# K and V products of a cross-attention by Strassen's scheme over pairs of batches

## The reference

```python
q = x @ Wq + bq
kv = context @ Wkv + bkv
k, v = jnp.split(kv, 2, axis=-1)
...
q = _larope(q, Lq)
k = _larope(k, Lk)
scores = jnp.einsum('bhqd,bhkd->bhqk', q, k) * SCALE
scores = jnp.where(context_mask[:, None, None, :], scores, -jnp.inf)
attn = jax.nn.softmax(scores, axis=-1)
out = jnp.einsum('bhqk,bhkd->bhqd', attn, v)
out = out.transpose(0, 2, 1, 3).reshape(B, Lq, H * hd)
return out @ Wo + bo
```

## Time and profile before

| | us |
|---|---|
| median of 3 runs | 776.84 (775.82 to 777.03) |
| the profiled execution | 779.38 |
| its span, first to last instruction | 777.6 |
| PE / DVE / ACT / POOL busy | 751.2 / 500.9 / 418.6 / 336.6 |
| mean granted TensorE clock | 0.985 of full speed |

### The profile page before, as it was taken

The page is one execution under the profiler, slowest core; times in us unless marked ns, Lnnn a source line. Parts: engine busy times, 40 slices in busy tenths (PEclk is TensorE's granted clock), DMA queues, the critical chain, the costliest instruction groups (busy, mean ns, idle before and its releaser), DMA issues. The chain is left out here.

```text
span 777.6 us, 23428 instructions
## 1 busy us (share of the span) xinstructions
PE 751.2 (97%) x9650; PEld 665.3 (86%) x9651; DVE 500.9 (64%) x1209; ACT 418.6 (54%) x978; POOL 336.6 (43%) x366
## 2 busy tenths in 40 slices
PE   8999999999999999999999999999899999599997
PEld 7899999999999999998999989997677777488784
DVE  6776765666575585675666557656889998622236
ACT  5465656556565566656656556664466664033330
POOL 1655456455454455544555445531133221246640
PEclk9989999999999999999999999999999999689999
DMA  8504010110011110011001100201942238634448
GB/s 294 208 29 164 27 40 29 36 57 30 29 36 36 49 37 29 32 33 57 30 29 49 44 30 29 83 29 57 408 174 110 105 122 350 207 114 166 162 140 319
DMA packets 23174, 77.96 MB, mean 100 GB/s; under 512 B 3328, under 2 KB 4736, under 8 KB 20128
## 3 DMA queue, kind: packets, MB, share of 16 engines
q1 hardware_dynamic: 19392, 64.45, 23.1%
q0 software_dynamic: 3680, 12.06, 4.7%
HBM read 57.89 MB, written 18.61 MB: 98 GB/s over the span
## 5 line engine op out<-in xcount | busy, mean ns | idle before, releaser
L164 PE MATMUL bank<-chi,wparts 128*128 128x258 f32 x496 | 143.2, 289 | 0.5 <-DVE v L759 0.5
L166 PE MATMUL bank<-chi,wparts 128*128 128x258 f32 x496 | 139.9, 282 | 0.0
L165 PE MATMUL bank<-clo,wparts 128*128 128x258 f32 x496 | 139.8, 282 | 0.0
L392 POOL TENSOR_TENSOR ksin<-kb,const 128x516 f32<-128x516 f32 x64 | 93.4, 1460 | 101.1 <-ACT kb L505 101.0
L505 ACT ACTIVATE kb<-bank,bias_cols 128x258 f32<-128x258 f32 x126 | 60.0, 476 | 66.4 <-PE bank L166 66.4
L412 POOL TENSOR_TENSOR ctx_sums<-craw 128x512 f32<-128x512 f32 x30 | 39.5, 1315 | 128.2 <-DVE ctx_sums_lo L776 128.2
L164 PEld LDWEIGHTS bank<-chi,wparts 128*128 128x128 f32 x496 | 93.8, 189 | 1.1 <-DVE v L759 0.7
L165 PEld LDWEIGHTS bank<-clo,wparts 128*128 128x128 f32 x496 | 94.1, 190 | 0.0
L166 PEld LDWEIGHTS bank<-chi,wparts 128*128 128x128 f32 x496 | 93.8, 189 | 0.0
L748 DVE TENSOR_TENSOR kcos<-kb,const 128x516 f32<-128x516 f32 x64 | 51.0, 798 | 29.6 <-ACT kb L505 29.6
L510 ACT ACTIVATE pr<-pr,nmax 128x257 f32<-128x257 f32 x128 | 63.5, 500 | 5.8 <-DVE nmax L784 5.8
(11 more groups left out here) (380 smaller groups left out, 2243.9 us busy)
## 6 DMA issues: line engine op xcount, KB each, us to landing
craw<-ctx_t_dram SPq DMA_DIRECT2D x32, 516.0 KB, 3.5
expert_lo<-weights_dram SPq DMA_DIRECT2D x8, 1024.0 KB, 12.5
expert_hi_scratch<-wraw SPq DMA_DIRECT2D x16, 512.0 KB, 2.7
wparts<-expert_hi_scratch SPq DMA_DIRECT2D x8, 1024.0 KB, 9.0
wraw<-weights_dram SPq DMA_DIRECT2D x7, 1024.0 KB, 5.8
expert_lo<-ffn_out_scratch SPq DMA_DIRECT2D x16, 256.0 KB, 5.8
x<-x_dram SPq DMA_DIRECT2D x8, 256.0 KB, 7.6
ffn_xn_scratch<-xn SPq DMA_DIRECT2D x8, 256.0 KB, 2.2
```

The source lines that it names most:

```text
L164: pe.matmul(psum, ahi(c), bhi(c), start=(c == 0), stop=False)
L165: pe.matmul(psum, ahi(c), blo(c), start=False, stop=False)
L166: last = pe.matmul(psum, alo(c), bhi(c), start=False, stop=(c == chunks - 1))
L392: pool.tensor_tensor(ksin[:, part, :], kb[:, part, :], sink[:, part, :], ALU.mult).then_inc(s_ksin, 1)
```

## The change

K and V of batches 4 to 31 are now made for pairs of batches. For both, Strassen's scheme takes the two batches as one direction of the 2 x 2 blocks, halves of the contraction as the second, halves of the output features as the third: 7 products in place of 8. The context blocks of a pair and their sums lie in one tile of seven parts (`ctx_parts_hi`, `ctx_parts_lo`), used by K and V alike; a K product is taken in two column blocks of 6 matmuls with 258 columns, a V product is 12 matmuls of 256 columns for 256 keys of a batch. Batches 0 to 3 are plain (`PLAIN` was 2). Even and odd steps now differ: an odd step makes most of K for the next pair, an even step the rest of V and the first of the K products of the pair after. In even steps the transposes of the probabilities stand behind the fourth V product. K's sums on DVE, the two-in-turn `kb`, weight sums for K (K's weights are loaded a second time for them) and other places for some tiles (`pr`, `pt` in x's later tiles and in `wraw`; so x tiles 3 to 7 are loaded after batch 7, and the weights of the self-attention to the context's tiles or later) come with it. PE, and of the others what the prediction speaks of:

```diff
-PLAIN = 2
+PLAIN = 4
...
+            K_PRODUCTS = ((0, 2), (0, 5), (0, 1), (0, 6), (0, 3), (0, 7), (1, 2), (1, 5), (0, 4), (1, 3), (1, 1), (1, 6),
+                          (1, 7), (1, 4))
+            V_PRODUCTS = (2, 5, 1, 6, 3, 7, 4)
...
+                    if n == AV:
+                        sp.wait_ge(s_kcos, trig_of(B - 1))
+                        sp.wait_ge(s_ksin, trig_of(B - 1))
...
+                    for i in range(2):
+                        sp.wait_ge(s_clo, i + 3 if q == PAIR_FIRST else parts_of(q - 1, O_T4))
+                        ctx(2 * q + i, i)
...
+                def ctx_sums_early(q):
...
+                    pool.tensor_tensor(t1_raw, craw[1][:, 0:2, :], craw[0][:, 0:2, :], ALU.subtract).then_inc(s_tr, 1)
+                    pool.wait_ge(s_tr, ctx_sum_of(q, R_T1))
+                    pool.tensor_tensor(craw[1][:, 0:2, :], craw[1][:, 2:4, :], craw[1][:, 0:2, :], ALU.subtract).then_inc(s_tr, 1)
...
+                def even_step(b, t, j):
+                    p, q = b // 2, b // 2 + 1
+                    more = q <= PAIR_LAST
+                    last = t == TILES - 1
+                    v_copy(p, 5)
+                    v_copy(p, 1)
+                    if more:
+                        part_hi(q, O_X1)
+                    exp(b, 0)
+                    exp(b, 1)
+                    v_copy(p, 6)
+                    exp(b, 2)
+                    exp(b, 3)
+                    if more:
+                        part_hi(q, O_22)
+                    next_mask(b)
+                    v_copy(p, 4)
+                    for g in range(G):
+                        pt_evac(b, g)
...
+                def last_step(b):
+                    for g in range(G):
+                        exp(b, g)
+                    before_o_hi(b)
+                    for g in range(G):
+                        pt_evac(b, g)
+                    act.wait_ge(s_vp1, v_product_of(PAIR_LAST, 4))
+                    w_hi(AV)
...
+                def k_sum(q, c, s):
+
+                    product, copied, psum = {S_11: (2, 1, two), S_12: (3, 6, plus), S_22: (7, 5, base)}[s]
+                    dve.wait_ge(s_proj, k_product_of(q, c, product))
+                    dve.wait_ge(s_kev, k_copy_of(q, c, copied))
+                    dst = kb_of(2 * q + (s != S_11))[:, c + 2 * (s == S_22), :]
+                    dve.tensor_tensor(dst, psum[:, 0:LKP], dst, ALU.add).then_inc(s_kd, 1)
...
+                def even_step(b, t, j):
+                    p, q = b // 2, b // 2 + 1
+                    more = q <= PAIR_LAST
+                    last = t == TILES - 1
+                    begin_step(b, j)
+                    v_sum(p, S_11)
+                    if more:
+                        part_lo(q, O_X1)
+                    v_sum(p, S_12)
+                    v_sum(p, S_22)
+                    o_sum(b - 1)
...
+                OPERANDS = {1: (F_11, B_11), 2: (F_12, B_21), 3: (F_S4, B_22), 4: (F_22, B_T4), 5: (F_S1, B_T1),
+                            6: (F_S2, B_T2), 7: (F_S3, B_T3)}
+
+                def bank_of(k):
+                    return two if k == 2 else plus if k in (3, 5) else base
...
+                    own = k in (1, 2, 5)
+                    for i in range(2):
+                        pe.matmul(psum, whi_i[:, i, cols], hi[:, i, :], start=own and i == 0, stop=False, skip_group_check=not own)
+                        pe.matmul(psum, wlo_i[:, i, cols], hi[:, i, :], start=False, stop=False, skip_group_check=not own)
+                        last = pe.matmul(psum, whi_i[:, i, cols], lo[:, i, :], start=False, stop=i == 1, skip_group_check=not own)
+                    last.then_inc(s_proj, 1)
...
+                def even_step(b, t, j):
+                    p, q = b // 2, b // 2 + 1
+                    more = q <= PAIR_LAST
+                    v_product(p, 6)
+                    v_product(p, 3)
+                    v_product(p, 7)
+                    if more:
+                        k_product(q, 0, 2)
+                    else:
+                        self_product(0)
+                    v_product(p, 4)
+                    probs_transposed(b)
+                    if more:
+                        k_product(q, 0, 5)
+                    extra_step(b, t, j)
+                    if more:
+                        k_product(q, 0, 1)
+                    diagonals_spread(b)
+                    attend(b, j)
+                    if more:
+                        k_product(q, 0, 6)
+
+                def odd_step(b, t, j):
+                    p = (b + 1) // 2
+                    k_product(p, 0, 3)
+                    k_product(p, 0, 7)
+                    k_product(p, 1, 2)
+                    k_product(p, 1, 5)
+                    probs_transposed(b)
+                    k_product(p, 0, 4)
+                    k_product(p, 1, 3)
+                    k_product(p, 1, 1)
+                    extra_step(b, t, j)
+                    k_product(p, 1, 6)
+                    v_product(p, 2)
+                    k_product(p, 1, 7)
+                    v_product(p, 5)
+                    k_product(p, 1, 4)
+                    diagonals_spread(b)
+                    attend(b, j)
+                    v_product(p, 1)
+
+                def last_step(b, j):
+                    self_product(1)
+                    probs_transposed(b)
+                    diagonals_spread(b)
+                    attend(b, j)
```

More of the change, by code:

```diff
@@ L447, in _ @@
                 pool.tensor_copy(same[:], const[:, C_SAME:C_SAME + P]).then_inc(s_same, 1)
[L448 to L462 removed]
+                k_sin_plain(0, 0)
@@ L477, in _ @@
-                body(0)
-                for t in range(1, TILES - 1):
-                    body(t)
-                body(TILES - 1, last=True)
+                        ln_and_bias(t, j)
+                        if b < B - 1:
+                            k_sin(b + 1, 2)
+                    else:
+                        for i in range(3):
+                            k_sin(b + 1, i)
+                        o_bias(b - 1)
+                        diagonals(b)
+                        if q <= PAIR_LAST:
+                            ctx_sums_late(q)
+                        ln_and_bias(t, j)
@@ L741, in q_rotate, with k_cos_plain @@
+                    dve.tensor_tensor(plain[:, :, 16:32], swap[:, :, 0:16], half(xn, odd), ALU.add)
+                    dve.tensor_tensor(swap[:, :, 0:16], swap[:, :, 0:16], half(xn, odd), ALU.add)
+                    dve.tensor_tensor(swap[:, :, 16:32], swap[:, :, 16:32], half(xn, even),
                                       ALU.subtract).then_inc(s_qr, 1)
-                def k_cos(b, half):
+                def k_cos_plain(b, half):
                     dve.wait_ge(s_kev, b * 4 + 2 * half + 2)
-                    if half == 0 and not at_start(b):
+                    if half == 0 and b > 0:
@@ L1050, in plain_v_product @@
                         last.then_inc(s_vp1, 1)
-                def v_product(psum, rows, block, start):
-                    (hi, lo), (whi_i, wlo_i) = rows, wv_block(block)
-                    for c in range(2):
-                        pe.matmul(psum, hi[:, c, :], whi_i[:, c, :], start=start and c == 0, stop=False, skip_group_check=not start)
-                        pe.matmul(psum, hi[:, c, :], wlo_i[:, c, :], start=False, stop=False, skip_group_check=not start)
-                        last = pe.matmul(psum, lo[:, c, :], whi_i[:, c, :], start=False, stop=c == 1, skip_group_check=not start)
-                    return last
@@ L1256, in _, with extra_step @@
-                body(0, first=True)
-                for t in range(1, TILES - 1):
-                    body(t)
-                body(TILES - 1, last=True)
+                def extra_step(b, t, j):
+                    if b == 0:
+                        v_last_product()
+                    elif j == 0:
+                        out_product(t - 1, b)
+                    if j == 1:
+                        xn_transposed(t + 1, b)
+                    if j == 2 and t < TILES - 1:
+                        q_product(t + 1, b)
+                    if j == 3 and t < TILES - 1:
+                        q_transposed(t + 1, b)
@@ new lines, in last_step @@
+                def last_step(b, j):
+                    self_product(1)
+                    probs_transposed(b)
+                    diagonals_spread(b)
+                    attend(b, j)
+                for b in range(B):
+                    t, j = divmod(b, BT)
+                    extra_free(t, j, t == 0, t == TILES - 1)
+                    scores(b, j)
+                    if b < PLAIN - 1:
+                        plain_step(b, t, j)
+                    elif b == B - 1:
+                        last_step(b, j)
+                    elif b % 2 == 0:
+                        even_step(b, t, j)
+                    else:
+                        odd_step(b, t, j)
```

1052 lines of the change are left out of this document (614 added, 438 removed).

## The result

832.0 us median of 4 runs (827.87 to 834.48) against 776.93 before: ratio 1.0703, 95% interval 1.0653 to 1.0752. The forecast was 778.8 with a range up to 789; the result lies 43 us above that end. The profiled execution, 827.87 us, is the quickest of the four; against the 779.38 of before it is +48.5 us where the sum said +2.0.

The account below looks back on a forecast made before the run. PE's own instruction stream was taken to set the length. Savings of 20.2 us against 1.4 + 1.4 + 4.3 + 6.1 + 2.7 + 1.7 + 1.3 + 3.3 summed to +2.0 on 776.84: 778.8 us, range 768 to 789.

Parts of the forecast that it names:

- Even batches, output or query product: PE waits there for all four copies of probabilities, 0.37 + 0.10 us in 13 batches: 6.1 us.
- DVE gains 6 x 258 of K sums: all in their idle 40%: DVE's added K sums, like ACT's copies, counted as covered by idle time and so at nothing.
- DVE and POOL block each other: Rival: one blocking more at V sums and K sums, 0.4 us twice a pair, 10.4 us: 789.2; chance 0.15.
- The third rival: Half clock behind the wait for self-attention's V weights at the end, 3.6 us: 782.4; chance 0.08.
- the 0.120 apart of the sum: K matmuls of 258 columns cost 0.120 us each on PE; fourteen pairs save 20.2 us.
- the 0.33 predicted: Even batches, fourth V product: PE waits 0.23 + 0.10 us for DVE's V sum in 13 batches, 4.3 us.
- 0.38 predicted: Odd batches, sixth product of the second K column block: wait behind the K copy in 7 of 14, 2.7 us.
- the 0.12: Odd batches, first product of the second K column block: 0.12 us with the restart, x 14, 1.7 us.
- 2.9 were predicted: PE's wait for self-attention's V weights at the end, 2.8 + 0.1 us, within an end term of 3.3 us.
- A dense product between attention and scores: Late second matmul behind the attention products, 0 to 0.10 us in each of 28 batches, middle taken: 1.4 us.
- The forecast's own case: Strassen's saving is given back as short PE waits and a little more: 778.8 us, 774 to 784; chance 0.52.
- The price of the later transposes alone, 10.4 predicted: Both even-batch waits, 4.3 and 6.1 us; the rival that they do not come gave 768.4, chance 0.25.

Follow-up runs that it names:

- Experiment one: Changed kernel with DVE's output low part ahead of the three K tables and the statistics, ACT's high part ahead of the fourth V copy in even batches; 794.4 us.
- experiment four: Changed kernel with POOL's two late context sums behind its share of the LayerNorm in even batches; 807.5 us.
- five to eight: Orders changed cumulatively on Experiment one: POOL's bias earlier; DVE's statistics, ACT's normalised rows later; transposes earlier; last output product before self-attention's V product; 793.5, 792.7, 791.8, 790.7 us.
- the seventh kernel: Experiment one plus POOL's bias earlier, DVE's statistics and ACT's normalised rows later, transposes of probabilities back ahead of the fourth V product; 791.8 us.
- the second experiment: Changed kernel with only the transposes of the probabilities and ACT's copies of them back ahead of the fourth V product in even batches; 829.4 us.
- experiment fourteen: As thirteen, but with the transposes of the probabilities and their copies behind the fourth V product; 781.9 us (1.0075).
- five to ten: The orders of five to eight; then, on the seventh kernel, DVE's K sums earlier in odd batches (785.8 us) and ACT's first K copy earlier in even ones (783.8 us).
- thirteen: As the twelfth, but in even batches DVE makes the output's low part ahead of the bottom-right context part and the sum; 775.26 us against 775.91 before (0.999).
- the tenth: The seventh kernel with DVE's second and third K sums earlier in odd batches and ACT's first K copy ahead of the fourth sum's high part in even ones; 783.8 us.
- the twelfth: As the tenth, with the last output product ahead of self-attention's V product, and DVE making the four context sums of every pair but the first; 779.6 us.

## Why the prediction was wrong

**The step that failed.** "*Even batches, output or query product.* It needs the bank of the fourth transposed group, so all four copies of probabilities." The output product has a second need, the low part of the last batch of its tile, which DVE makes within the same step. The prediction named what the product's *bank* waits for and not what its *operand* waits for. It walked ACT's queue there, and not DVE's, and so had no term for this wait, which measured 4.4 us seven times, with 1.9 us of half clock behind each. The 2.9 us of K and V products that lay ahead of the product in before are not what kept it away: PE comes to the product only 0.8 us sooner now. What kept it away was DVE's order, with the low part ahead of the statistics and the tables, and the change put it behind them. Experiment one, which puts it ahead again, takes the wait out.

**What made it dear.** "DVE gains 6 x 258 of K sums: all in their idle 40%" counted added work against an average and left out that the order had changed. At that place DVE was busy for 4.92 of 5 us. Had it used the durations without POOL, the low part would still have been late by some 2 us (experiment four).

**The rival that was half right.** *DVE and POOL block each other* had the mechanism, and its 789.2 lies near the 790 to 794 of experiments one and five to eight. Its place was wrong: it looked at the V and K sums, at 0.4 us a time. The blocking fell on the tables (969 and 1782 ns for 446 and 746) and on `otlo`, in the queue ahead of a wait that it had not listed. The Trainium skill (SBUF — State Buffer, Who interferes with whom) says that a DVE instruction with two SBUF inputs contends with a POOL instruction that reads SBUF, and that the shared pair of ports is an exclusive lock. The trace agrees: in the seventh kernel's rows a table ends 0.28 us and a low part 0.14 us behind POOL's instruction.

**The clock.** The third rival looked for half clock at the end only. It came there too: behind a wait of 3.25 us eight of the V product's eleven distances are 0.39 to 0.43 us, some 1.6 us lost for the 3.6 it priced. But it came seven times more in the middle.

**What held.** K's products take 0.72 us for six matmuls, the 0.120 apart of the sum. The fourth V product waits 0.23 us, and its second matmul comes 0.10 late (the restart): the 0.33 predicted. The query product (j = 2) waits 0.45, with a restart of 0.08: 0.47 predicted. In odd batches the sixth product of the second column block starts 0.37 us late where only the transposes of the normalised rows cover it, for 0.38 predicted, and the first product of that block has a restart of 0.10 to 0.11 us in each of the 13, for the 0.12. PE waits 3.25 us for the V weights at the end where 2.9 were predicted. Two of these stand in the changed kernel's trace (PE: from the K product behind the seventh V product to the fourth V product; the wait ahead of self-attention's V product):

```profile
176.98 0.28 PE L1358 MATMUL bank<-ctx_parts_lo,wparts 128*128 128x258 f32 x1
177.34 0.39 PE L1381 MATMUL bank<-wparts,ctx_parts_hi 128*128 128x256 f32 x1
177.56 0.28 PE L1383 MATMUL bank<-wparts,ctx_parts_hi 128*128 128x256 f32 x1
...
585.28 0.50 PE L167 MATMUL bank<-wparts,xthi 128*128 128x512 f32 x1 [3.25 <-DVE wparts L878]
585.61 0.59 PE L168 MATMUL bank<-wparts,xthi 128*128 128x512 f32 x1
```

From 176.98 to 177.34 are 0.36 us where 0.12 is the spacing, and 0.22 to the next matmul.

**Terms mis-sized, all small.** A dense product between attention and scores costs 0.17 us in an even batch (six matmuls) and 0.14 in an odd one (twelve), not 0.05: six matmuls to the scores' start take 0.92 us, 0.2 over, less 0.03 by which they start sooner than the scores did. That is some 4.3 us for 1.4. In odd batches the seventh product of the second K column block and the fifth V product wait for copies and sums, 0 to 1.1 us a step, some 3 us in all 13; the sum had no term for them. Half clock at 40 to 45 us is absent in the changed kernel's profiled execution (1.00), where the first attention product comes 2.8 us sooner (44.0 for 46.8); in the second experiment's it was there again (0.50). That is luck of one execution.

**The forecast's own case** is experiment fourteen, nearly: the scheme, the order of its transposes and no late low part, but also the sums on DVE and the other changes of order of five to ten. It takes 781.9, a little slower than before, where the prediction had 778.8 within 774 to 784. The price of the later transposes alone, 10.4 predicted, measures 9.1 in the even steps and 6.6 in all.

Without that price the sum says 768.4, and thirteen takes 775.3. In its profiled execution the 25 steps between the attentions of batches 3 and 28 take 391.4 us for 400.5 before, 9.1 less, where K's 12.5 pairs x 1.44 save 18.0. The other 9 are, nearly, the dense products (3.9), the sixth K product's start (2.2), the wait of j = 1 (2.2) and the late second matmuls (1.2).

## What to carry to other kernels

When a change takes work from the bottleneck, list for each instruction that remains every operand and buffer it waits for, and walk the queue of each engine that makes one, in the step where it is made; an engine's free share over the span says nothing about the place of one short instruction in its line. Compare each engine's order with that of the kernel before: an instruction that is only moved can cost more than all that is added. An instruction that a later engine needs goes ahead of longer work in the same queue that nobody waits for yet. Where two engines lengthen each other's instructions, price the queue with the durations under that load.

## What was not expected of the hardware

Behind a wait of some 2.2 us PE ran at its lower clock in four of seven like steps and at full clock in three (experiment four, matmuls 0.43 and 0.23 us apart); a wait of 4.4 us cost another 1.9 us of half clock behind it. Moving four sums from POOL to DVE, the busier of the two, made the kernel some 3 us faster: DVE's 258-column tables of the even batches took 1505 ns in the changed kernel and 929 in the tenth, with the sums on POOL, and 415 ns in the twelfth, with them on DVE.
